# Attention probabilities turned through DRAM: one return transfer of 128 partitions for four of 32, a transpose of every fourth column, and rounding and splitting in instructions of 1024 elements

## What is computed

```python
# layer 0: graph attention over the adjacency, concat, residual, layernorm
x = _layernorm(x + _L0_gnn_ref(x, adj, W, a))
# layer 1: 8-head attention, head size 64, masked by adj, float32
q, k, v = (split_heads(x @ Wi.T + bi) for Wi, bi in ...)
scores = einsum('bhqd,bhkd->bhqk', q, k) / 8;  scores[adj == 0] = -inf
attn = softmax(scores)
x = _layernorm(x + (attn @ v).merge_heads() @ Wo.T + bo)
```

## Time and profile before

| | us |
|---|---|
| median of 3 runs | 3178.0 |
| lowest, highest | 3174.58, 3180.0 |
| profiled execution, its span | 3177.6 |
| PE busy | 2986.1 (94%) |
| DVE busy | 2630.0 (83%) |
| ACT busy | 2481.0 (78%) |
| POOL busy | 2079.3 (65%) |
| DMA queue of SP, share of 16 engines | 75.0% |

### The profile page before, as it was taken

One profiled execution on the slowest core, in us unless ns is written; L12 is line 12 of the kernel. 1 busy time (PEld: TensorE's weight loads), 2 busy tenths in 40 slices (PEclk: granted clock), 3 DMA queues, 4 the chain that ended last, 5 costly groups with the idle time before them and its releaser, 6 DMA issues.

```text
span 3177.6 us, 60582 instructions
## 1 busy us (share of the span) xinstructions
PE 2986.1 (94%) x19084; PEld 2513.6 (79%) x19084; DVE 2630.0 (83%) x6553; ACT 2481.0 (78%) x5543; POOL 2079.3 (65%) x1927
## 2 busy tenths in 40 slices
PE   5899999999999999999999999999999999999995
PEld 4788888887888887788887887887888877888874
DVE  4788888888888888888888888888888888888874
ACT  3778788777788877888778887777888877888764
POOL 1566676666766666766667766666766666766664
PEclk7999999999999999999999999999999999999997
DMA  3677887777877777887777787777777778877765
GB/s 123 193 220 220 222 230 221 212 218 208 232 231 222 216 218 205 232 230 219 215 215 218 225 235 207 214 212 221 224 228 223 212 216 223 228 221 223 206 198 148
DMA packets 290047, 681.92 MB, mean 215 GB/s; under 512 B 40512, under 2 KB 74048, under 8 KB 256960
## 3 DMA queue, kind: packets, MB, share of 16 engines
q1 hardware_dynamic: 289728, 678.05, 75.0%
HBM read 375.40 MB, written 302.51 MB: 213 GB/s over the span
## 4 chain that ended last, share of the span: by engine, by line
PE 42%; DMA 25%; POOL 9%; DVE 8%; ACT 8%; SPq 3%; issue 3%; ACTq 0%; DVEq 0%; POOLq 0%
PE R_bank L724 27%; DMA turned_lo_prob<-scratch 12%; DMA scratch<-blocked 9%; PE O_bank L813 8%; POOL turned_lo_prob L1163 7%; PE S_bank L794 5%; DVE blocked L1105 3%; DMA r_wide<-r_scratch 3%; ACT turned_hi_prob L841 3%; SPq L628 3%; PE L_bank L715 2%; ACT prob L927 2%; POOL o_half L1158 1%; DVE qk_pair L1002 1%; ACT o_half L946 1%
## 5 line engine op out<-in xcount | busy, mean ns | idle before, releaser
L1163 POOL TENSOR_TENSOR turned_lo_prob<-turned_lo_prob,turned_hi_prob 128x512 fp32r<-128x512 f32 x1024 | 1297.1, 1297 | 564.0 <-ACT turned_hi_prob L841 563.2
L927 ACT ACTIVATE prob<-prob,small_cols 128x512 f32<-128x512 f32 x1024 | 729.8, 714 | 152.2 <-DVE small_cols L1085 143.9
L841 ACT ACTIVATE turned_hi_prob<-turned_lo_prob 128x512 fp32r<-128x512 f32 x1024 | 596.6, 622 | 228.1 <-DMA turned_lo_prob<-scratch 218.4
L1105 DVE STREAM_TRANSPOSE blocked<-prob 128x512 f32<-128x512 f32 x1024 | 692.4, 695 | 76.3 <-ACT prob L927 40.3
L1085 DVE CUSTOM_DVE_ANT_0 prob<-S_bank,mask 128x512 f32<-128x512 f32 x1024 | 677.2, 680 | 24.1 <-PE S_bank L794 20.1
L813 PE MATMUL O_bank<-turned_hi_prob,v_st 128*128 128x256 f32 x2048 | 528.2, 294 | 86.9 <-POOL turned_lo_prob L1163 83.6
L813 PE MATMUL O_bank<-turned_lo_prob,v_st 128*128 128x256 f32 x2048 | 513.6, 287 | 0.0
L813 PEld LDWEIGHTS O_bank<-turned_hi_prob,v_st 128*128 128x128 f32 x2048 | 398.3, 195 | 136.8 <-POOL turned_lo_prob L1163 125.3
L794 PE MATMUL S_bank<-qk_pair 64*128 64x512 f32 x3072 | 445.6, 416 | 16.3 <-DVE small_cols L1085 9.3
L724 PE MATMUL R_bank<-wv,x1T 128*128 128x256 f32 x3072 | 401.3, 286 | 1.6 <-DVE v_st L984 1.5
L813 PEld LDWEIGHTS O_bank<-turned_lo_prob,v_st 128*128 128x128 f32 x2048 | 399.6, 195 | 3.4
(11 more groups left out here) (90 smaller groups left out, 4390.0 us busy)
## 6 DMA issues: line engine op xcount, KB each, us to landing
scratch<-blocked SPq DMA_DIRECT2D x256, 1024.0 KB, 4.6
turned_lo_prob<-scratch SPq DMA_DIRECT2D x1024, 256.0 KB, 5.5
tokens<-xT SPq DMA_DIRECT2D x128, 256.0 KB, 4.8
tokens<-x SPq DMA_DIRECT2D x128, 256.0 KB, 3.8
r_wide<-r_scratch SPq DMA_DIRECT2D x512, 64.0 KB, 3.4
out<-tokens SPq DMA_DIRECT2D x128, 256.0 KB, 4.0
r_scratch<-r_cols SPq DMA_DIRECT2D x256, 2.0 KB
tokens<-adj SPq DMA_DIRECT2D x1, 1024.0 KB, 6.5
```

The lines of the kernel that those rows point to most:

```text
L841: act.activation(dst, src, ACT.Copy).then_inc(done, 1)
L927: act.activation(prob_tile(R, s), prob_tile(R, s), ACT.Exp, bias=negmax[:, slot:slot + 1], scale=-1.0, accum_out=psum_row[:, ph % 2, j:j + ...
L1105: dve.transpose(blocked[:, ph % 2, :, :, 2 * (s % 2) + s % 4 // 2, :].rearrange("p d c i -> p c d i"), prob_tile(R, s).rearrange("p (c d i ...
L1163: pool.tensor_tensor(turned_lo_prob[:, ph % 2, a, :, :], turned_lo_prob[:, ph % 2, a, :, :].bitcast(F32), turned_hi_prob[:, a, :, :].bitca ...
```

## The change

1. `turn_blocks` views the tile as `p (c i d)`: block `d` of a chunk now takes every fourth column, `d`, `d + 4`, `d + 8` and so on. The written side is as before. The transpose then reads floats that lie 4 elements (16 bytes) apart.
2. `scratch` is laid out so that key `4 j + d` of chunk `c` is row `4 j + d`. `store_probs` still writes one run of 8 KB a partition, and `load_probs` is one transfer over 128 partitions, again with four runs of 2 KB a partition. The four semaphores of a phase parity become one.
3. `probs_hi` and `probs_lo` take two quarters at once, 1024 elements a partition; there are 16 of each a graph, and `weigh` waits for two `lo` a phase instead of four.
4. In the plans of ACT and POOL every second `hi` and every second `lo` is struck out. The plans of PE, DVE and SP stay.

```diff
 SCALAR_PLAN = (
     "exp pre1 hi C0",
-    "hi hi exp exp",
-    "hi exp exp aexp1",
-    "lows hi pre2 hi",
-    "hi hi exp exp",
+    "hi exp exp",
+    "exp exp aexp1",
+    "lows hi pre2",
+    "hi exp exp",
...
 GPSIMD_PLAN = (
     "norm turn",
-    "lo lo",
-    "lo lo",
+    "lo",
+    "lo",
...
-"hi": (32, 0), "lo": (32, 0)
+"hi": (16, 0), "lo": (16, 0)
...
-        scratch = nc.dram_tensor("scratch", [4, P, 4 * N], F32, kind="Internal").ap()
+        scratch = nc.dram_tensor("scratch", [4, 4, P, N], F32, kind="Internal").ap()
...
             def store_probs(R, ph):
                 if due(R.n(8, ph - 3)):
-                    for d in range(4):
-                        sp.wait_ge(*moved(R, ph - 4, d))
+                    sp.wait_ge(*moved(R, ph - 4))
                 sp.wait_ge(p_turned, R.n(32, 4 * ph + 4))
-                sp.dma_start(scratch[ph % 4, :, :],
+                sp.dma_start(scratch[ph % 4, :, :, :].rearrange("a (j d) x -> (a j) (d x)", d=4),
                              blocked[:, ph % 2, :, :, :, :].rearrange("p d c j i -> p (d c j i)")).then_inc(p_stored[ph % 2], 16)
 
             def load_probs(R, ph):
                 sp.wait_ge(*stored(R, ph))
-                by_key_block = scratch[ph % 4, :, :].rearrange("(a j) (d x) -> d j a x", a=4, d=4)
-                for d in range(4):
-                    sp.dma_start(turned_lo_prob[BLK * d:BLK * (d + 1), ph % 2, :, :, :].rearrange("p a c x -> p a (c x)").bitcast(F32),
-                                 by_key_block[d]).then_inc(moved(R, ph, d)[0], 16)
+                sp.dma_start(turned_lo_prob[:, ph % 2, :, :, :].rearrange("p a c x -> p a (c x)").bitcast(F32),
+                             scratch[ph % 4, :, :, :].rearrange("a p x -> p a x")).then_inc(moved(R, ph)[0], 16)
...
             def weigh(R, g):
-                pe.wait_ge(p_lo, R.n(32, 4 * ph + 4))
+                pe.wait_ge(p_lo, R.n(16, 2 * ph + 2))
...
             def probs_hi(R, m):
-                ph, a = m // 4, m % 4
+                ph, a = m // 2, m % 2
                 if a == 0 and due(R.n(16, 2 * ph)):
                     act.wait_ge(pv_mm, R.n(16, 2 * ph))
                 if a == 0:
-                    for d in range(4):
-                        act.wait_ge(*moved(R, ph, d))
-                split_hi(turned_hi_prob[:, a, :, :], turned_lo_prob[:, ph % 2, a, :, :].bitcast(F32), p_hi)
+                    act.wait_ge(*moved(R, ph))
+                split_hi(turned_hi_prob[:, 2 * a:2 * a + 2, :, :], turned_lo_prob[:, ph % 2, 2 * a:2 * a + 2, :, :].bitcast(F32),
+                         p_hi)
...
                 dve.transpose(blocked[:, ph % 2, :, :, 2 * (s % 2) + s % 4 // 2, :].rearrange("p d c i -> p c d i"),
-                              prob_tile(R, s).rearrange("p (c d i) -> p c d i", c=T, i=BLK)).then_inc(p_turned, 1)
+                              prob_tile(R, s).rearrange("p (c i d) -> p c d i", c=T, i=BLK)).then_inc(p_turned, 1)
...
             def probs_lo(R, m):
-                ph, a = m // 4, m % 4
-                pool.wait_ge(p_hi, R.n(32, m + 1))
-                pool.tensor_tensor(turned_lo_prob[:, ph % 2, a, :, :], turned_lo_prob[:, ph % 2, a, :, :].bitcast(F32),
-                                   turned_hi_prob[:, a, :, :].bitcast(F32), ALU.subtract).then_inc(p_lo, 1)
+                ph, a = m // 2, m % 2
+                pool.wait_ge(p_hi, R.n(16, m + 1))
+                lo_ap = turned_lo_prob[:, ph % 2, 2 * a:2 * a + 2, :, :]
+                pool.tensor_tensor(lo_ap, lo_ap.bitcast(F32), turned_hi_prob[:, 2 * a:2 * a + 2, :, :].bitcast(F32),
+                                   ALU.subtract).then_inc(p_lo, 1)
```

More of the change, by code:

```diff
@@ L97 @@
     "lap2 E0 turn hi",
-    "E1 hi lows hi",
-    "hi E2 lap3 exp",
+    "E1 lows hi",
+    "E2 lap3 exp",
     "E3 exp exp turn",
     "exp evV0 evV1 A1",
-    "hi hi hi B0",
-    "exp lows hi exp",
+    "hi hi B0",
+    "exp lows exp",
     "exp exp evQ4 turn",
-    "lows A2 hi hi",
+    "lows A2 hi",
     "B1 hi evV2 exp",
-    "evV3 hi exp exp",
+    "evV3 exp exp",
     "A3 turn B2 exp",
-    "exp lows hi hi",
-    "hi hi turn B3",
+    "exp lows hi",
+    "hi turn B3",
     "exp",
@@ L148 @@
     "norm turn",
[L149 to L152 removed]
+    "lo",
+    "lo",
+    "lo",
+    "lo",
     "yrs norm",
[L154 removed]
+    "lo",
     "turn lo",
[L156 removed]
+    "norm",
     "turn lo",
[L158 to L159 removed]
+    "lo",
+    "lrs",
     "A0 norm",
     "bo0 turn",
[L162 to L163 removed]
+    "lo",
+    "lo",
     "norm turn",
     "A1 lo",
[L166 to L167 removed]
+    "lo",
+    "norm",
     "turn bo1",
     "A2 lo",
[L170 to L171 removed]
+    "lo",
+    "norm",
     "A3 turn",
     "norm lo",
[L174 to L175 removed]
+    "lo",
+    "turn",
     "bo2 bo3",
@@ L219 @@
     "evQ1 exp exp lows turn",
-    "exp hi hi hi exp",
-    "hi exp exp exp hi",
-    "hi hi lows hi exp",
+    "exp hi hi exp",
+    "exp exp exp hi",
+    "hi lows exp",
     "exp turn evQ2 exp hi",
-    "hi hi hi evW0 lows",
+    "hi evW0 lows",
     "evW1 exp exp exp exp",
     "turn evW2 lows evW3 hi",
-    "hi exp hi exp hi",
+    "exp hi exp",
     "evQ3 exp exp turn hi",
-    "hi hi hi exp exp",
+    "hi exp exp",
     "exp lows fin0 exp exp",
[L231 to L235, removed]
+    "fin1 turn fin2 hi",
+    "hi lows exp exp",
+    "exp hi hi turn",
+    "fin3 lows turn hi",
+    "hi lows turn",
 )
@@ L257 @@
     "norm turn lo",
[L258 to L272, removed]
+    "lo",
+    "lo lo",
+    "norm turn",
+    "lo lo",
+    "norm turn",
+    "lo lo",
+    "norm yrs",
+    "turn lo",
+    "lo norm",
+    "turn lo",
+    "lo norm",
+    "lo turn",
+    "lo norm",
+    "turn lo",
+    "lo norm",
     "turn",
@@ L298 @@
               sv B2 evV3 scores scores vt vt exp q1 inv bo2 reduce reduce A3 exp exp exp B3 bo3"""
-UNITS = {"scores": (16, 4), "reduce": (32, 6), "inv": (8, 1), "exp": (32, 6), "norm": (8, -1), "vt": (32, 4), "mv": (8, 0), "hi": (32, 0), "lo": (32, 0), "weigh": (16, -2), "lows": (8, -1), "sum": (8, -1), "turn": (8, -1), "sv": (8, 1), "rs": (8, 1), "rl": (8, 0)}
+UNITS = {"scores": (16, 4), "reduce": (32, 6), "inv": (8, 1), "exp": (32, 6), "norm": (8, -1), "vt": (32, 4), "mv": (8, 0), "hi": (16, 0), "lo": (16, 0), "weigh": (16, -2), "lows": (8, -1), "sum": (8, -1), "turn": (8, -1), "sv": (8, 1), "rs": (8, 1), "rl": (8, 0)}
 ENDING = """norm weigh lows sum evO0 evO1 turn weigh yst0 evO2 yst1 yst2 fin0 evO3 fin1 O0 yst3 O1 O2 O3 fin2 yrs
@@ L494, in graph_layers @@
         bias_hi, bias_lo, bias_mm, bias_done = sem("bias_hi"), sem("bias_lo"), sem("bias_mm"), sem("bias_done")
-        p_moved = [[sem(f"p_moved{i}{a}") for a in range(4)] for i in range(2)]
+        p_moved = [sem(f"p_moved{i}") for i in range(2)]
         p_stored = [sem(f"p_stored{i}") for i in range(2)]
```

12 lines of the change are left out of this document (6 added, 6 removed).

## The result

The changed kernel takes 3233.69 us (median of 4 runs, 3231.99 to 3240.13), the kernel before 3176.29 us (3172.37 to 3180.0) beside it: 1.018 times as long [1.016, 1.0199], 57 us more. The forecast was 3435. The sign holds, and the size, +257 us, is four and a half times too large. That 3234 lies between 3115 and 3510 is no merit: the range was made wide for rival 1, and the forecast's own case began at 3345.

A forecast was written before the change was run, and what follows sets the result against it. PE was taken as the bound, then DVE: 840.2 + 329 x 0.54 + 8.4 = 1026 us, at 96% full 1069 for 984, so +256 us; 3177.6 + 256 + 4 = 3438, stated as 3435, range 3115 to 3510.

The forecast's parts named there:

- rival 1: Transpose's step is free and the shorter return pays: 3138 us, ends 3100 to 3172; chance 0.36.
- the forecast's own case: Stepped transpose makes DVE the bound: 3435 us, its own range 3345 to 3560; chance 0.50.
- What bounds the kernel now: In the middle 2978 us PE bounds, busy 96.6% of the window; DVE has 144 us in 984 to spare.
- The return: Probabilities' load as one transfer lands in 5.5 us, 2 us less in a leg of 7.6 (1.3 to 3.0).
- Rounding and splitting: `hi` on ACT and `lo` on POOL at 1024 elements take 1.05 and 2.40 us; costed at nothing.
- Longer holds by POOL: Longer `lo` instructions make DVE wait 27 us more in all, 8.4 us in the 984 us window.
- The transpose: On DVE, one more slot per element read 16 bytes apart: 0.54 us more, 1.23 us a tile.
- PE needs 950 and cannot hide that; DVE bounds the kernel.: Middle window: DVE's 1026 us exceeds the old 984; at 96% full it takes 1069 us, 8.6% more.
- The signs: Profile after: transposes 1.2 us with no idle before, DVE 94 to 97%, PE under 90% and waiting for `reduce`.
- Rival 3: Step is free; coarser `hi` delays `exp` and the tiles behind it, 55 us: 3233 us; chance 0.03.
- Rival 2: Transpose's step costs half a slot, 0.27 us; DVE 95% beside PE 96.6%: about 3240 us; chance 0.07.
- Rival 4: Return lands no sooner, saving 1 us or nothing; with a free step 3178 us; chance 0.04.

The follow-up runs named there:

- return_only: Kernel before with only the one-transfer return over 128 partitions, contiguous transpose and 512-element instructions kept (keys on wrong partitions, same work): 3102.5 us, ratio 0.9759.

## Why the prediction was right on the sign and wrong on the size

- **What bounds the kernel now**: PE, but not alone. The view that misled was PE's 96.6% in the window: it hid that the transfers carry 25% of the chain of waits. I had read that chain for one phase, not its shares. In return_only they fall to 1%, PE has 85% of the chain and the time falls by 76 us.
- **The return.** The landing was right: 5.6 us, 5.5 forecast. The value was wrong: this step failed. In the forecast's own sum it is worth nothing in the middle and 12 us in the last graph; rival 1 gave it -28 and -12. Alone it is -76, and beside the step, where the transfers have 22% of the chain, it is worth -86 (3320.2 to 3234.6).
- **Rounding and splitting** at nothing: right. 1.052 and 2.434 us were forecast as 1.05 and 2.40; their effect is 0 to -5 us.
- **Longer holds by POOL**, +27 us on DVE: half right and of no use. The coarser grain lengthens the mask addition by 166 ns (900 to 1066) and, beside the step, by 227 (804 to 1031). But the tiny instruction went from 639 ns to 306 with the return alone and to 239 in all, which the forecast did not have; the two groups come to 143 us for 145.
- **The transpose: this step failed.** "I take one more slot for each element", 0.54 us, was an assumption from no row, and it measured 0.40 us. Of the 201 us between 3435 and 3234 this is the largest term. With 0.40 in the forecast's own sum, 840.2 + 329 x 0.40 + 8.4 = 980 us of DVE, 980 / 0.96 = 1021, 3.8% of 2978 is 112, so 3290: 145 us of the 201. The 8.4 us of longer holds, which did not come, are 26 more. DVE itself is busy only 358 us longer in all for the transposes' 409: the busy times of its groups together rise by 398, and instructions that follow each other without a gap overlap at their ends.
- **"PE needs 950 and cannot hide that; DVE bounds the kernel."** This step failed too, though the window ends where it said, with DVE at 95.0%. Were the fuller engine the only bound, the kernel before with the step on every second tile, DVE at 87%, would cost little for PE at 96.6%, and beside the step the return would be worth nothing. Measured: +70 and -86. Each microsecond by which the stepped transposes lengthen DVE's busy time costs 0.37 to 0.39 of a microsecond at each dose (70 of 190, 142 of 365, 136 of 353); at the evictions of `q` and `k` it is some 0.2 (16 of 76).
- **The signs.** DVE's 95.0% was forecast, as 94 to 97. PE under 90% did not come (95.1% of the window), nor did PE's waits for `reduce` (9.0 us for 9.3), and the transposes still have 38.1 us idle before them, for 76.3. A PE that stays so full speaks against DVE as the only bound.
- **The rivals.** **Rival 3** has the measured time, 3233, by luck: its step is free and its grain costs 55 us, where the step costs 142 and the grain nothing. **Rival 2** (half a slot, 3240) is as near, with 0.27 us where 0.40 is true and with nothing for the return: two errors that cancel. **Rival 1** had the sign of the return and half its size, and a free step. **Rival 4** is out by return_only.

That the added work acts by delaying handoffs to ACT and PE at the place where it stands is argued from the dose and the waits, and it is not shown; no run took the handoffs apart, nor PE's longer busy time.

## What to carry to other kernels

Price a stepped operand before building on it, and look first whether the step can stand in a PSUM read that is there anyway: here that turned +57 us into -65, but only in the version that left the plans and the masks alone; three others with stepped PSUM reads took 60 to 98 us more than the kernel before. Read the chain's shares by engine, not one stretch of it: transfers at a quarter of the chain were worth 76 us beside an engine at 96.6%. Give each transfer 128 partitions, and on both sides the long dimension outermost (128 rows landed in 4.1 us, four block rows in 13).

## What the runs showed of the hardware that was not expected

- A transpose that reads SBUF in steps of 2 floats pays nothing (712 ns for 712), and in steps of 4 it pays 0.38 us in 512 floats, no more at 16 (1049 ns). A step of 4 costs the same in DVE's additions (686 to 1054 ns read, 751 to 1118 written) and more on ACT (722 to 1216). In PSUM, reads in steps of 4 are free on both, and reads in steps of 16 (680 ns) and 32 (682 ns) on DVE. The Trainium skill's sentence on lines of 16 bytes and two hits (SBUF — State Buffer, "Door 1: The DMA port swizzle") agrees with the place of the break; its reading that 4 fp32 are free does not.
- Four 256 KB stores with 4 block rows outermost on the DRAM side have their last one land after 13 us, at 0.32 of the DMA engines; one of 1 MB with 128 rows outermost lands after 4.1.
- A 256 KB load onto 128 partitions lands after 3.5 us, and one onto 32 partitions after 5.5 us; the median packet of 2 KB takes 84 ns beside the first and 136 ns beside the second. With the same packets and bytes the queue takes 62.7% of the DMA engines for 75.0%.
- 2 us in which PE was busy 0.50 us were followed by a granted clock of 0.51 for 2 us and 0.63 for the next 2.
